# The B products of all segments on diagonals: TensorE multiplies delta u with diag(B), which ScalarE (three of four) and GpSimd (one of four) make

## What is computed

```python
delta = softplus(xp[..., :64] @ dt_proj_w + dt_proj_b)      # (B, S, 256)
Bm, Cm = xp[..., 64:80], xp[..., 80:]                       # (B, S, 16) each
dA  = exp(delta[..., None] * A)                             # (B, S, 256, 16)
dBu = delta[..., None] * Bm[:, :, None, :] * u[..., None]   # (B, S, 256, 16)
def step(h, inp):                                           # over the 1024 positions
    dA_t, dBu_t, C_t = inp
    h = dA_t * h + dBu_t
    return h, einsum('bdn,bn->bd', h, C_t)
y = ys + u * D_skip
```

## Time and profile before

| | us |
|---|---|
| median of 3 runs | 759.8 (757.31 to 759.98) |
| the profiled execution, device time | 758.83 |
| its span, first to last instruction | 756.2 |
| first scan to the end of the last scan | 64.0 to 535.6 |
| experts and the rest | 535.6 to 756.2 |

### The profile page before, as it was taken

How to read it: one execution, slowest core, us unless ns; L and a number is a source line. 1 busy time by engine, 2 the same in 40 slices (tenths; PEclk the granted TensorE clock), 3 DMA queues, 4 the chain that set the end, 5 groups by cost and what they waited for, 6 DMA issues and landing times.

```text
span 756.2 us, 14740 instructions
## 1 busy us (share of the span) xinstructions
PE 639.5 (85%) x4563; PEld 537.0 (71%) x4563; DVE 551.7 (73%) x1170; ACT 538.6 (71%) x1024; POOL 542.3 (72%) x519
## 2 busy tenths in 40 slices
PE   3768899989888989988988985899688997899994
PEld 3334766867857767766776774889577886899983
DVE  5066779899888998987989988999544574365552
ACT  3167989979987997996997997868226644465640
POOL 3055979989899899999999999978615454544431
PEclk9999999999999999999999999999789999999997
DMA  6020345355534633643344433586011122222544
GB/s 218 2 112 2 95 111 151 100 155 185 165 97 122 166 96 97 170 118 101 91 122 125 128 94 96 150 224 160 23 34 55 56 61 59 65 67 63 151 151 146
DMA packets 72492, 82.93 MB, mean 110 GB/s; under 512 B 7088, under 2 KB 63472, under 8 KB 68320
## 3 DMA queue, kind: packets, MB, share of 16 engines
q1 hardware_dynamic: 66944, 70.78, 34.6%
q0 software_dynamic: 4320, 9.12, 3.5%
q10 hardware_dynamic: 1152, 2.10, 0.7%
HBM read 52.19 MB, written 29.78 MB: 108 GB/s over the span
## 4 chain that ended last, share of the span: by engine, by line
PE 41%; ACT 32%; DVE 10%; issue 9%; POOL 3%; another core or an unknown queue 2%; DMA 2%; SPq 0%; ACTq 0%; DVEq 0%; POOLq 0%
PE psum L567 24%; PE psum L571 16%; ACT S L976 11%; ACT dA L987 10%; DVE ring L1335 4%; POOL ring L542 1%; ACT xn L881 1%; ACT L916 1%; ACT soft L908 1%; ACT soft L916 1%; ACT soft L909 1%; ACT L987 1%; ACT u L886 1%; ACT hT L863 1%
## 5 line engine op out<-in xcount | busy, mean ns | idle before, releaser
L542 POOL TENSOR_TENSOR ring<-ring,Cb 128x1024 f32<-128x1024 f32 x128 | 302.9, 2368 | 15.7 <-DVE ring L1335 10.4
L987 ACT ACTIVATE dA<-delta,A 128x512 f32<-128x512 f32 x256 | 178.6, 716 | 12.1 <-DVE ring L1335 12.0
L571 PEld LDWEIGHTS psum<-ident,S 128*128 128x128 f32 x896 | 107.4, 145 | 109.9 <-issue 75.8
L571 PE MATMUL psum<-ident,S 128*128 128x128 f32 x896 | 142.1, 284 | 45.8 <-issue 24.6
L571 PE MATMUL psum<-ident,ring 128*128 128x128 f32 x1088 | 164.5, 283 | 12.4 <-DMA ring<-results 6.7
L1335 DVE TENSOR_TENSOR_SCAN ring<-dA,state,psum 128x512 f32<-128x512 f32 x128 | 158.0, 1266 | 1.4 <-PE psum L571 1.0
L1335 DVE TENSOR_TENSOR_SCAN ring<-dA,psum 128x512 f32<-128x512 f32 x128 | 150.6, 1207 | 10.8 <-PE psum L571 6.8
L976 ACT ACTIVATE S<-duT,BT 128x256 f32<-128x256 f32 x320 | 139.3, 502 | 26.5 <-DVE duT L1078 17.8
L559 POOL DMA_INDIRECT results<-xn,result_at x71 | 68.7, 968 | 108.7 <-DVE xn L1462 68.1
L571 PEld LDWEIGHTS psum<-ident,ring 128*128 128x128 f32 x1088 | 132.7, 147 | 14.2 <-DMA ring<-results 7.4
L567 PE MATMUL psum<-uT,S 128*128 128x128 f32 x852 | 109.7, 280 | 0.5 <-issue 0.5
(11 more groups left out here) (229 smaller groups left out, 835.6 us busy)
## 6 DMA issues: line engine op xcount, KB each, us to landing
Cb<-c_rows SPq DMA_DIRECT2D x32, 1024.0 KB, 6.0
token_rows<-zeros SPq DMA_DIRECT2D x64, 272.0 KB, 7.0
uT<-token_rows SPq DMA_DIRECT2D x71, 68.0 KB
ring<-results SPq DMA_DIRECT2D x16, 256.0 KB, 3.4
xT<-in_xT SPq DMA_DIRECT2D x4, 512.0 KB, 5.2
out_T<-xT ACTq DMA_DIRECT2D x8, 256.0 KB
stage<-in_xT SPq DMA_DIRECT2D x6, 256.0 KB, 8.3
gateup_w<-in_gate SPq DMA_DIRECT2D x1, 1408.0 KB, 9.3
```

The source lines that it names most:

```text
L542: nc.gpsimd.tensor_tensor(ring[:, k % RING], ring[:, k % RING], Cb[:, group_ % 2, own, :].unsqueeze(1).to_broadcast([P, HALVES, BANK]), AL ...
L571: return nc.tensor.matmul(out, block_in, ident[at, at], is_transpose=True, start=start, stop=True, skip_group_check=True)
L987: nc.scalar.activation(dA[:, (k * HALVES + a) % DA_SLOTS, :], delta[:, s % 2, a, :], ACT.Exp, scale=A[:, a, n:n + 1]).then_inc(da_ready, 1)
```

## The change

`turn_in` uses the form of segment 7 in all segments: for each chunk it multiplies `duT` (128 positions x 128 channels of half a) with a 128 x 128 diagonal that holds B. `S` holds only these diagonals, 128 columns for a chunk instead of 256, and has 6 slots in the same memory. In every step of every segment ScalarE makes three of the four diagonals and GpSimd the fourth (`POOL_CHUNKS = 1`). `scale_in` no longer waits for duT; `turn_in` does, at the first step of a segment, each half for its own. VectorE waits before it overwrites `duT` until the products of the segment before last are done. The counts of the semaphores follow.

```diff
--- before.py
+++ after.py
@@ -25,7 +25,8 @@
 LN_EPS = 1e-5
 PROJ = DTRANK + 2 * NSTATE
 GAPS = 2 * NSTATE
-RING, S_SLOTS, DBU_BANKS, DA_SLOTS, C_GROUP, LAG = 6, 3, 3, 6, 4, 3
+RING, S_SLOTS, DBU_BANKS, DA_SLOTS, C_GROUP, LAG = 6, 6, 3, 6, 4, 3
+POOL_CHUNKS = 1
 
 INNER = [(c * P, min(P, INTER - c * P)) for c in range(-(-INTER // P))]
 NIN = len(INNER)
@@ -48,21 +49,6 @@
 def wait(eng, signal, count):
     if not (isinstance(count, int) and count <= 0):
         eng.wait_ge(signal, count)
-
-
-def pool_chunks(k):
-
-    s = k // NSTATE
-    return 1 + k % 2 if s < 2 else int(s < SEGS - 1)
-
-
-def act_scaled(k):
-
-    return sum(CS - pool_chunks(j) for j in range(k + 1))
-
-
-def pool_scaled(k):
-    return sum(pool_chunks(j) > 0 for j in range(k + 1))
 
 
 def adaln_kernel(nc, xT_d, w1_d, w2_d, wo_d, xproj_d, dtw_d, alog_d, conv_d, cols_d, bo_d, router_d,
@@ -143,7 +129,7 @@
         soft = sb("soft", [P, 3, HALVES, BANK])
         rv, ev, lw = (soft[:, k] for k in range(3))
         delta = sb("delta", [P, 2, HALVES, BANK])
-        S = sb("S", [P, S_SLOTS, CS, MLP])
+        S = sb("S", [P, S_SLOTS, CS, P])
         dA = sb("dA", [P, DA_SLOTS, BANK])
         Cb = sb("Cb", [P, 2, C_GROUP, BANK])
         ring = sb("ring", [P, RING, HALVES, BANK])
@@ -513,15 +499,12 @@
 
             def scale_in(k):
                 s, n = divmod(k, NSTATE)
-                own = pool_chunks(k)
-                if own:
-                    if n == 0:
-                        pool.wait_ge(read["bt"], s + 1)
-                        pool.wait_ge(read["dT1"], s + 1)
-                    wait(pool, turned_in, HALVES * (k - S_SLOTS + 1))
-                    nc.gpsimd.tensor_tensor(S[:, k % S_SLOTS, CS - own:, :], duT[:, s % 2, CS - own:, :],
-                                            BT[:, s % 2, CS - own:, n:n + 1].to_broadcast([P, own, MLP]), ALU.mult
-                                            ).then_inc(scaled_pool, 1)
+                if n == 0:
+                    pool.wait_ge(read["bt"], s + 1)
+                wait(pool, turned_in, HALVES * (k - S_SLOTS + 1))
+                nc.gpsimd.tensor_tensor(S[:, k % S_SLOTS, CS - 1, :], ident[:, :],
+                                        BT[:, s % 2, CS - 1, n:n + 1].to_broadcast([P, P]), ALU.mult
+                                        ).then_inc(scaled_pool, 1)
 
             pool.wait_ge(mod_step, MOD_STEPS)
             for window in (-2, -1):
@@ -701,17 +684,16 @@
             def turn_in(k, a):
 
 
+                s, n = divmod(k, NSTATE)
+                if n == 0:
+                    pe.wait_ge(read[f"dT{a}"], s + 1)
                 if a == 0:
-                    pe.wait_ge(scaled_act, act_scaled(k))
-                    pe.wait_ge(scaled_pool, pool_scaled(k))
+                    pe.wait_ge(scaled_act, (CS - POOL_CHUNKS) * (k + 1))
+                    pe.wait_ge(scaled_pool, k + 1)
                 wait(pe, scanned, HALVES * k + a - DBU_BANKS + 1)
-                s = k // NSTATE
                 for c in range(CS):
-                    if s < SEGS - 1:
-                        last = turn(db(k, a)[:, c * P:(c + 1) * P], S[:, k % S_SLOTS, c, a * P:(a + 1) * P])
-                    else:
-                        last = product(db(k, a)[:, c * P:(c + 1) * P], duT[:, s % 2, c, a * P:(a + 1) * P],
-                                       S[:, k % S_SLOTS, c, 0:P])
+                    last = product(db(k, a)[:, c * P:(c + 1) * P], duT[:, s % 2, c, a * P:(a + 1) * P],
+                                   S[:, k % S_SLOTS, c, :])
                 last.then_inc(turned_in, 1)
 
             def add_state(k, a):
@@ -899,7 +881,7 @@
             def project(gap, f):
                 if gap == 12:
                     act.wait_ge(filled["bt"], f + 1)
-                    wait(act, scaled_pool, pool_scaled((f - 1) * NSTATE - 1))
+                    wait(act, scaled_pool, (f - 1) * NSTATE)
                     nc.scalar.copy(BT[:, f % 2].rearrange("p c n -> p (c n)"), FB[:, 0:CS * NSTATE]).then_inc(read["bt"], 1)
                 if gap in (5, 8):
                     a = (gap - 5) // 3
@@ -969,15 +951,10 @@
                 s, n = divmod(k, NSTATE)
                 if n == 0:
                     act.wait_ge(read["bt"], s + 1)
-                    act.wait_ge(read["dT1"], s + 1)
                 wait(act, turned_in, HALVES * (k - S_SLOTS + 1))
-                for c in range(CS - pool_chunks(k)):
-                    if s < SEGS - 1:
-                        nc.scalar.activation(S[:, k % S_SLOTS, c, :], duT[:, s % 2, c, :], ACT.Identity,
-                                             scale=BT[:, s % 2, c, n:n + 1]).then_inc(scaled_act, 1)
-                    else:
-                        nc.scalar.activation(S[:, k % S_SLOTS, c, 0:P], ident[:, :], ACT.Identity,
-                                             scale=BT[:, s % 2, c, n:n + 1]).then_inc(scaled_act, 1)
+                for c in range(CS - POOL_CHUNKS):
+                    nc.scalar.activation(S[:, k % S_SLOTS, c, :], ident[:, :], ACT.Identity,
+                                         scale=BT[:, s % 2, c, n:n + 1]).then_inc(scaled_act, 1)
 
             def decay(k, a):
                 s, n = divmod(k, NSTATE)
@@ -1073,8 +1050,7 @@
                     dve.wait_ge(filled[f"dT{a}"], f + 1)
                     dve.wait_ge(read[f"uT{a}"], f + 1)
                     if f > 1:
-                        dve.wait_ge(scaled_act, act_scaled((f - 1) * NSTATE - 1))
-                        dve.wait_ge(scaled_pool, pool_scaled((f - 1) * NSTATE - 1))
+                        dve.wait_ge(turned_in, HALVES * (f - 1) * NSTATE)
                     V.tensor_tensor(duT[:, f % 2, :, a * P:(a + 1) * P], uT[:, :, a * P:(a + 1) * P],
                                     FB.rearrange("p (c d) -> p c d", c=CS), ALU.mult).then_inc(read[f"dT{a}"], 1)
```

## The result

The changed kernel takes 798.0 us in the median of 4 runs (797.7 to 798.2), beside 759.9 for the kernel before: a ratio of 1.050, 95% interval 1.047 to 1.053. The forecast was 809 in a range of 785 to 833. The span of the profiled execution grew from 756.2 to 795.5 us, by 39.3.

A forecast was written before the change was run, and what follows sets the result against it. No engine was full in segments 1 to 5; TensorE's extra products would make it the bound. Segments +53, clock -5 and GpSimd +1.6 gave +50 on the profiled 758.8 us: 809 us, range 785 to 833.

The forecast's parts named there:

- The price of a product: In TensorE's groups of four, segments 0 to 6: products take 0.89 us for transposes' 0.44, 14.5 us more a segment.
- TensorE as the bound of segments 1 to 5: Segments 1 to 5: TensorE has no idle left, each lasts its earlier busy time plus 14.5 us, together +41.5.
- the clock: TensorE in segments 0 and 2 to 6: half the loss from slow stretches comes back, -0.9 us each, -5 in all.
- rival C: TensorE's earlier busy time includes modelled ends before pauses, some 3 us a segment not work: 788 us; 88% together with the forecast.
- Segments 0 and 6: Before the clock's gain: segment 0 grows by 6.6 us, segment 6 by 5, mostly in its two first quarters.
- ScalarE's relief at nothing: ScalarE's smaller scalings save up to 5.7 us a segment, counted as nothing because TensorE's 14.5 us cover it.
- GpSimd's diagonals: Segment 7: 0.40 us a step, 6.4 us in all, of which four scalings after 518.31 add 1.6 us to the path.
- one of my signs: End of the scans: the last scatter would come 1 to 3 us further behind the last scan.
- The moved wait for duT, VectorE's new wait and the deeper ring: The wait moved to turn_in, VectorE's wait before overwriting duT and the deeper S ring: no time gained or lost.
- A: Segments 0 to 6: by weight loads TensorE has room, others' relief shows, 746 us; deciding point 0.63 us a group; chance 3%.
- B: Segments 0 to 6: TensorE keeps its waits, every new 0.45 us is on the path, about +95, 854 us; chance 7%.
- D: Whole kernel: no change, because something else hides the cost of segment 7's form; chance 2%.

## Why the prediction was right, point by point

**The price of a product** (0.89 us a group for 0.44): right to the hundredth. That was known because the last segment already ran the changed form. (32 x 0.45 is 14.4 us a segment, where I wrote 14.5.)

**TensorE as the bound of segments 1 to 5**: right. I forecast +41.5 us, less 0.9 each for the clock in segments 2 to 5, so +37.9. Measured are +29.9. The term that was mis-sized is TensorE's busy time of before, which I took as work. Two parts of it were not. First the clock: I expected half of its loss back, and all of it came, 1.00 for 0.97, which is 0.9 us a segment more. Then the modelled ends before pauses, my rival C. Segment 1 shows them alone, because its clock was 1.00 before: 66.7 forecast, 65.1 measured, so 1.6 us. In segments 2 to 5, with all of the clock's 1.8 us (my estimate) taken off, 0.6 to 0.8 us are left. Rival C put them at 3 us a segment, from some 20 pauses of 0.16 us; the trace before has 5 to 7 pauses of TensorE in each of these segments, so 0.8 to 1.1 us by the same price. Each of the two parts was named in the prediction; I gave the one half of its size and kept the other out of the sum.

**Segments 0 and 6**: forecast +5.7 and +4.1 with the clock, measured +2.8 and +2.5. The same term is at fault. In segment 0 I took 47.1 us as TensorE's work, and with the products it is busy for 58.2 us, all of the segment and 11.1 more, not 14.5. Of the 3.4 us some 1.7 are the clock, 0.97 before and 1.00 now. The other 1.7 are about what the modelled ends are in segment 1. The 0.4 us that I added for a stretch in its middle, in which the norm is waited for, did not show. That stretch, the third quarter, took 20.4 us at a clock of 0.92 and takes 17.0 without a pause of TensorE:

```profile
90.00:107.00 17.00, 17.00 (x131) 14.79 (x129) 14.46 (x17) 16.81 (x34) 12.67 (x14) 1.00 0.36 95
```

For segment 6 I had taken +5 by judgement, about 2 us in each of the first two quarters and a little in the last. The first two grew by 1.3 and 2.9 us, but the last went from 14.2 us to 12.6. With four doubled transposes and no relief of the others it takes 14.0, so here the relief showed.

**ScalarE's relief at nothing**: right (it is busy 50.2 us in segment 3, where I named 48), shown by 793.5 us without it and 794.6 with it, but for about 1 us in segment 6. With TensorE at its old price the relief of both engines was worth 11.8 us in segments 0 to 6, within the up to 5.7 us a segment that I named.

**GpSimd's diagonals**: priced at 0.40 us, measured 0.402. In segment 7 I put +1.6 us on the path, four scalings behind GpSimd's last idle time, and the early part of the 6.4 us into its idle time. The stretch behind it grew by 1.5 us, as forecast. The early part did not quite fit: 0.5 us in segment 6 and 0.6 in segment 7 ahead of that stretch reached the scatter too, together 2.6 us. The path that I named, through GpSimd's program to the last scatter, was the right one. What I did not see is that TensorE would wait for a diagonal behind a scatter and so end the scans 4.6 us later. That made one of my signs fail: the last scatter starts 2.9 us behind the last scan (578.92 for 576.0), not 1 to 3 us further than the 5.5 of before, because the last scan moved more than the scatter. It cost the kernel nothing that the runs show.

**The moved wait for duT, VectorE's new wait and the deeper ring**, all costed at nothing: right. TensorE has no pause at the starts of segments 1 to 5, and three slots give the same time as six. VectorE's wait had no run of its own.

**The rivals.** A (TensorE has room) fell. Its point of decision, some 0.2 us more a group, is where time begins to show, though: 0.11 us a group cost 2.0 us and 0.22 cost 8.5. It rested on the weight loads' busy share, which the Trainium skill, "Perfetto Trace Analysis", section "Identifying the Most-Contended Engine", recommends for judging TensorE's headroom. The trace does not agree. The share reads 57.6 of 66.3 us, 87%, in segment 5, in which TensorE never stops. In segment 3 before it was 72%, which looked like 17 us of room where there were some 9: the 66.2 us of segment 3 less 14.5 are 51.7 us of real work in 60.4. The matmuls' busy 54.2 erred by 2.5 us, and to the other side. Here it was the better measure. B (every 0.45 us on the path, +95 us) fell: TensorE kept none of its waits in segments 0 to 5. D (no change) fell with A.

The sum then, to the last scatter: +29.9 for segments 1 to 5, +5.3 for 0 and 6, +2.0 in segment 7, +0.6 ahead of the scans and +1.5 behind the scatter make +39.3 us, where I had +50. Nearly all of the difference is in segments 0 to 6, 35.2 us for 48: TensorE's busy time of before was taken as work.

## What to carry to other kernels

When four engines are within 10% of each other, price a move of work on the engine that receives it first, by the distance between starts of that same form elsewhere in the trace. The mean duration of a record, here 278 ns for a product's and 284 for a transpose's, hides that an fp32 product is two records where a transpose is one. Take TensorE's present work from such distances too: its busy time also holds the stretches at half clock and the modelled ends before pauses. Move only as much as the receiver has spare, and only from the engine that is last there: one chunk of four on a diagonal won 1%, all four lost 5%. Before you price a delay, ask which event the next stage waits for: here the last scan moved by 4.6 us in segment 7 and the scatter, which counted, by 2.0.

## What was not expected of the hardware

- The clock came back with little: 1.00 in segments 0 and 2 to 5 for 0.97, an estimated 1.8 us a segment. TensorE did not have to be without pauses for it. With one doubled transpose its longest pause in segment 3 was 1.68 us (282.50) and the clock stayed at 1.00. In the kernel before it was 2.10 us (281.13) and half clock followed. The run with transposes for products has 1.00 there too, with no more work of TensorE than before.
- One wait of 2.4 us in segment 7 was followed by groups at half speed (1.91 us for 1.06) and a granted clock of 0.89 for the quarter.
- Weight loads of a TensorE that never stops fill 87% of the time in this mix (57.6 of 66.3 us), not all of it.
- ScalarE takes 0.325 us for 128 columns in a row of three and 0.435 for 256, so half the columns save a quarter of the time; GpSimd 0.40 and 0.62.
